# Edge scores of a graph kernel leave the gather ring by DMA beside the row store, where ScalarE copied them

## What is computed

```python
feat_all = einsum('ni,rhid->rnhd', inputs, conv_weights)
el = sum(feat_all[edge_type, edge_src] * attn_l[edge_type], -1)
er = sum(feat_all[edge_type, edge_dst] * attn_r[edge_type], -1)
e  = leaky_relu(el + er, 0.2)
alpha = softmax of e over the edges of one destination
h  = segment_sum(alpha[..., None] * feat_src_e, edge_dst) + h_bias
...
x = layernorm(x + L0(x)); x = layernorm(x + L1(x)); x = layernorm(x + L2(x)); x = layernorm(x + L3(x))
```

## Time and profile before

| | us |
|---|---|
| median of 3 runs | 2039.0 (2038.72 to 2039.45) |
| the profiled execution | 2046.73 |
| its span, first to last instruction | 2045.0 |
| first gather, last gather (start) | 157.4, 1001.2 |
| GpSimd busy | 523.6 |
| VectorE busy | 1154.6 |
| ScalarE busy | 779.0 |
| TensorE matmul busy | 1467.7 |

### The profile page before, as it was taken

The page is one execution under the profiler, slowest core; times in us unless marked ns, Lnnn a source line. Parts: engine busy times, 40 slices in busy tenths (PEclk is TensorE's granted clock), DMA queues, the critical chain, the costliest instruction groups (busy, mean ns, idle before and its releaser), DMA issues.

```text
span 2045.0 us, 22094 instructions
## 1 busy us (share of the span) xinstructions
PE 1467.7 (72%) x5398; PEld 742.5 (36%) x5398; DVE 1154.6 (56%) x2998; ACT 779.0 (38%) x1163; POOL 523.6 (26%) x517
## 2 busy tenths in 40 slices
PE   6895888755545555555239999798998789889640
PEld 3443544110001010010128777554444344544430
DVE  5404443777767677776599988752261350530636
ACT  1332433655545555555110000035773337156021
POOL 0005344556646656666400000000000000000022
PEclk9995555655555555555559999898999989999875
DMA  3534333445544444544509888200000100000022
GB/s 143 170 141 139 128 113 121 148 145 165 163 133 148 154 143 154 171 152 154 170 28 314 273 273 268 78 1 22 1 1 1 31 0 1 1 1 1 11 57 61
DMA packets 74860, 223.92 MB, mean 109 GB/s; under 512 B 17384, under 2 KB 26516, under 8 KB 74260
## 3 DMA queue, kind: packets, MB, share of 16 engines
q1 hardware_dynamic: 50804, 158.00, 21.7%
q0 software_dynamic: 23968, 64.77, 11.8%
HBM read 140.09 MB, written 82.63 MB: 109 GB/s over the span
## 4 chain that ended last, share of the span: by engine, by line
PE 39%; DVE 13%; issue 6%; DVEq 2%; ACT 1%; POOL 1%; DMA 0%; another core or an unknown queue 0%; SPq 0%; POOLq 0%
PE bank L1673 14%; PE bank L1612 11%; PE bank L1693 2%; PE bank L1745 2%; PE bank L1657 2%; DVE arena L1079 1%; DVE arena L1037 1%; PE bank L1742 1%; DVE adjacency L1044 1%; DVE arena L1038 1%; PE bank L1731 1%; PE bank L1641 1%; POOL arena L523 1%; PE bank L1756 1%; ACT arena L605 1%
## 5 line engine op out<-in xcount | busy, mean ns | idle before, releaser
L523 POOL DMA_INDIRECT arena<-feat_table,arena x469 | 486.8, 1038 | 456.7 <-issue 240.4
L1554 PE MATMUL bank<-arena 128*128 128x480 f16 x586 | 336.6, 575 | 270.8 <-DVE arena L1038 161.1
L605 ACT ACTIVATE arena<-bank 128x480 uint16<-128x480 f32 x586 | 332.6, 572 | 274.9 <-PE bank L1554 172.6
L1044 DVE TENSOR_TENSOR adjacency<-adjacency,arena 128x480 uint16 x586 | 235.7, 402 | 131.8 <-issue 90.8
L1673 PE MATMUL bank<-arena 128*128 128x472 f16 x1440 | 294.9, 369 | 12.0 <-DVE arena L1228 8.1
L531 POOL DMA_INDIRECT arena<-al_table,edge_ends x15 | 14.5, 965 | 977.9 <-DMA al_table<-arena 973.7
L1554 PEld LDWEIGHTS bank<-arena 128*128 128x128 f16 x586 | 60.8, 104 | 546.8 <-DVE arena L1038 283.7
L1612 PE MATMUL bank<-arena 128*128 x966 | 229.3, 393 | 0.8 <-issue 0.3
L1673 PEld LDWEIGHTS bank<-arena 128*128 128x128 bf16 x1440 | 142.7, 99 | 164.4 <-issue 18.4
L1038 DVE TENSOR_SCALAR arena<-iota,arena 128x480 f16<-128x480 f16 x586 | 201.4, 344 | 0.0
L1612 PEld LDWEIGHTS bank<-arena 128*128 128x128 f32 x966 | 175.3, 191 | 55.1 <-issue 33.2
(11 more groups left out here) (291 smaller groups left out, 1533.6 us busy)
## 6 DMA issues: line engine op xcount, KB each, us to landing
edge_rows<-arena SPq DMA_DIRECT2D x67, 910.0 KB
arena<-edge_rows SPq DMA_DIRECT2D x117, 520.0 KB, 4.6
feat_table<-arena SPq DMA_DIRECT2D x60, 260.0 KB, 2.1
arena<-feat_table,arena POOLq DMA_INDIRECT x469
arena<-in_w SPq DMA_DIRECT2D x1, 2048.0 KB, 9.7
arena<-in_xT SPq DMA_DIRECT2D x1, 1920.0 KB, 18.2
arena<-in_x SPq DMA_DIRECT2D x1, 1792.0 KB
xt_table<-arena SPq DMA_DIRECT2D x3, 528.0 KB, 3.2
```

The lines of the kernel that those rows point to most:

```text
L523: g.indirect_dma_start(out=SLOT[k][:, j, :], out_offset=None, in_=feat_t, in_offset=bass.IndirectOffsetOnAxis(ap=IE[:, GB * b + j:GB * b + ...
L605: a.activation(EV[st % AS].rearrange("p r k -> p (r k)"), PS[4 + st % 4][:, 0:R2 * KW], ACT.Copy)\
L1044: v.tensor_tensor(dst, dst, EV[st % AS], ALU.add).then_inc(s["a_add"], 1)
L1554: mm(PS[4 + st % 4][:, 0:R2 * KW], OHS[st % AS], OHK[st % AS], start=True, stop=True).then_inc(s["a_mm"], 1)
```

## The change

ScalarE's `collect` and all its calls are gone, with the numbers that spread them. For each batch SyncE issues, ahead of the row store and behind the same wait, a DMA that takes the 4 score columns of the slot (128 partitions x 7 pieces of 16 bytes) straight into `SUM`. Both DMAs count on one semaphore a slot, so each batch adds 32, and the helper `moved(k, batches)` tells what slot `k` has reached when so many batches have gone through. GpSimd waits for that alone, TensorE's two waits ahead of the lane groups and VectorE's ahead of the weighing become waits on the three slots' semaphores, and the first row load waits for the end of the step-score stage, `sc_mm`, where it waited for `collected`.

```diff
-GC_ER, GC_ET, GC_LOOP = 10, 2, 62
...
+        def moved(k, batches):
+
+            return 32 * ((batches + NSLOT - 1 - k) // NSLOT)
...
             for b in range(NGB):
                 k = b % NSLOT
                 sp.wait_ge(g_done[k], BATCH * (b // NSLOT + 1))
+                sp.dma_start(SUM[:, GB * b:GB * (b + 1), :], SLOT[k][:, :, D:FW]).then_inc(r_st[k], 16)
                 sp.dma_start(rows_b[:, GB * b:GB * (b + 1), :], SLOT[k]).then_inc(r_st[k], 16)
 
             for k in range(NSLOT):
-                sp.wait_ge(r_st[k], 16 * ((NGB + NSLOT - 1 - k) // NSLOT))
+                sp.wait_ge(r_st[k], moved(k, NGB))
...
                 if b == 0:
-                    sp.wait_ge(s["collected"], NGB)
+                    sp.wait_ge(s["sc_mm"], SC)
...
                 if b >= NSLOT:
-                    pool.wait_ge(r_st[k], 16 * (b // NSLOT))
-                    pool.wait_ge(s["collected"], b - NSLOT + 1)
+                    pool.wait_ge(r_st[k], 32 * (b // NSLOT))
...
-            def collect(b):
-
-                act.wait_ge(g_done[b % NSLOT], BATCH * (b // NSLOT + 1))
-                a.activation(SUM[:, GB * b:GB * (b + 1), :], SLOT[b % NSLOT][:, :, D:FW], ACT.Copy).then_inc(s["collected"], 1)
...
-                if g % 3 == 0 and g:
-                    collect(g // 3 - 1)
...
-                if c % 2:
-                    collect(GC_ER + c // 2)
...
-                    due = GC_ER + GC_ET + (GC_LOOP - GC_ER - GC_ET) * (AU * n + u + 1) // (A_N * AU)
-                    while got < due:
-                        collect(got)
-                        got += 1
...
-            pe.wait_ge(s["collected"], B_EARLY)
+            for k in range(NSLOT):
+                pe.wait_ge(r_st[k], moved(k, B_EARLY))
             pe.wait_ge(s["pool_link"], 3)
             for g in range(GR):
                 if g == G_EARLY:
-                    pe.wait_ge(s["collected"], NGB)
+                    for k in range(NSLOT):
+                        pe.wait_ge(r_st[k], moved(k, NGB))
```

More of the change, by code:

```diff
@@ L324, in build @@
         names = """bias_ready turn_cols kb_mm ld_rec ld_w0 ld_xt ld_at ld_e3 consts fields idx_mm idx_ev vl_done tab_mm tab_ev tab_st feat_mm
-            feat_ev diag_done bc_mm sel_free collected cmp_done ws_mm selr_ready djr_mm sel_ready fld_mm fld_ev steps_done a_oh a_mm a_ev a_add
+            feat_ev diag_done bc_mm sel_free cmp_done ws_mm selr_ready djr_mm sel_ready fld_mm fld_ev steps_done a_oh a_mm a_ev a_add
             pool_link lane_mm lane_ev flags_in flags_mm tail_ready tail_mm cin_ready cin_mm exp_ready exp_done
@@ L338, in build @@
         g3 = [sem(f"rows_gathered{i}") for i in range(len(GROUPS))]
-        r_st = [sem(f"rows_stored{i}") for i in range(NSLOT)]
+        r_st = [sem(f"rows_and_scores_moved{i}") for i in range(NSLOT)]
         REL = S3.rearrange("p a b -> p (a b)")[0:1, 0:RBLK - NRB].bitcast(I32)
@@ L609, in _ @@
                 a_evac(0, st)
-            got = GC_ER + GC_ET
             for n in range(A_N):
@@ L613, in _ @@
                     a_evac(n, AS + u)
-                    due = GC_ER + GC_ET + (GC_LOOP - GC_ER - GC_ET) * (AU * n + u + 1) // (A_N * AU)
-                    while got < due:
-                        collect(got)
-                        got += 1
             for st in range(AS + A_N * AU, STEPS):
                 a_evac(0, st)
-            for b in range(got, B_EARLY):
-                collect(b)
             for g in range(GR):
-                if g == G_EARLY:
-                    for b in range(max(got, B_EARLY), NGB):
-                        collect(b)
                 act.wait_ge(s["lane_mm"], g + 1)
@@ L1148, in _ @@
             for k in range(NSLOT):
-                dve.wait_ge(r_st[k], 16 * ((NGB + NSLOT - 1 - k) // NSLOT))
+                dve.wait_ge(r_st[k], moved(k, NGB))
             for i in range(RGRP):
```

## The result

| | before | after |
|---|---|---|
| median | 2039.2 us (2038.7 to 2048.1) | **2446.0 us** (2443.3 to 2448.2, 4 runs) |
| span of the profiled execution | 2045.0 | 2445.0 |
| last gather (start) | 1001.2 | 787.8 |
| first and last product of the key stage | 167.5, 344.3 | 165.9, 903.9 |
| first and last add of the count loop | 369.0, 979.2 | 928.2, 1390.5 |

The ratio is 1.198, with an interval of 1.195 to 1.202. The sign and the mechanism were as forecast (rival A), but the time is 176 us above the 2270 forecast and outside the range of 2020 to 2320. The key stage did 0.37 matmuls per us beside the train, where the sum took 1.35.

What follows compares the result with a forecast made beforehand. Gathers ended last, 17 us over the count loop; unbroken, they would slow the key stage to 723 and start the loop at 759: +237, rounded to +231, on the 2039.0 median gives 2270 us, range 2020 to 2320.

Steps and rivals of the forecast that it cites:

- rival A: The forecast itself: any unbroken gather train slows key stage and count loop until it ends; 2225 to 2320 us, chance 0.58.
- the sum: Second L1106 moves from 1007.3 to 1244: +237 us, rounded to +231 and added to the median of 2039.0.
- The bound and the mechanism: Gathers end last, 17 us over the count loop; waits for ScalarE break the trains and let other engines' sequencers recover.
- ScalarE's copies at nothing: Removing 67 copies on ScalarE, 14.6 us in all, was counted as no gain because ScalarE doesn't pace the loop.
- score transfers under cover: 67 added transfers on SyncE's queue: 10.2 us per slot against 17.5 available, so GpSimd shouldn't wait.
- The train's end, 743.7: 469 gathers at 1.25 us each from 157.4, landed at 747; at 1.33 us each, 784.
- The key stage's pace, 1.35 per us between 1.2 and 1.56: TensorE beside the train: 743 products left at 173 take 550 us, to 723.
- The loop's 2.3 us a step: Count loop's pace in slow stretches beside gathers: 19 steps in 44 us.
- Within about 2 us of the end of the run they are on time again: Count loop: VectorE's late steps recover about 2 us after a run of three gather batches, about 28 us, ends.
- my own last sentence: The forecast is wrong above all if a long train lets TensorE's sequencer recover.
- The loop and the rest: Count loop after the train: 440 us of steps plus 35 of turns, 759 to 1234, then 10.4 us to the second L1106.
- Rival C: Slow stretches don't grow with the train and come as often as now until gathers end at 747; 1970 us, chance 0.20.

Runs made afterwards that it cites:

- paced_2: Changed kernel, GpSimd also waiting ahead of a batch until ScalarE's ordinary work reached where `collect` stood; 2044.2 us against 2042.0 before on chip 6.
- train_beside_loop: Changed kernel with the first gather held until the key stage is done, so the train lies beside the count loop; 2377.6 us against 2047.0 before on chip 10.

## Why the prediction was wrong in size, point by point

- **The bound and the mechanism: right.** GpSimd gathers in one train without waiting for anyone, TensorE's key stage takes 738 us with idle time called "issue", and the loop has no slow stretch. paced_2 shows that nothing else in the change counts. That the sign came out right was also luck: on chips 5 and 14 kernels with this train were faster than before (1849 and 1842 us against 1892), and no row of one trace could tell on which sort of chip the result would be taken.
- **ScalarE's copies at nothing, score transfers under cover: right.** GpSimd never waited for a slot by the profile, and without the transfers the time is 4 us less.
- **The train's end, 743.7: 44 us early.** 1.25 us per gather was the cadence in short windows; over the train it is (787.8 - 155.8) / 468 = 1.35, just past my upper end of 1.33.
- **The key stage's pace, 1.35 per us between 1.2 and 1.56: the step that failed.** It was 0.37. With 229 of 743 matmuls done by 788, 514 were left. The nine microseconds that priced it were the first of a slow stretch, before the pace had settled; both bounds came from the same nine, so the range was no bound at all. The loop's 2.3 us a step has the same fault (5.0 measured in train_beside_loop), but didn't enter the sum of the forecast, in which no step of the loop lies beside the train.
- **"Within about 2 us of the end of the run they are on time again": wrong for a long train.** After the last gather at 787.8 TensorE goes on as before until 808; its next rows (and behind the x20 it is at pace):

```profile
808.11 0.17 PE L1501 MATMUL bank<-arena 128*128 x1 [2.62 <-issue]
815.95 0.61 PE L1487 MATMUL bank<-adjacency,ident 128*128 128x512 f16 x1 [7.67 <-DVE arena L978]
...
818.27 2.61 PE L1501 MATMUL bank<-arena 128*128 x20
```

  It is on time again at 816, 28 us after the gathers. In train_beside_loop VectorE's steps stay 4 to 6 us apart from 931.0 until 956.9, 26 us. Part of this time no DMA runs at all (796 to 807 in the changed kernel: four products in 11 us at 0 GB/s):

```profile
796.00:807.00 11.00, 0.68 (x4) 0.52 (x5) 0.00 (x0) 0.00 (x0) 0.00 (x0) 0.50 0.00 0
```

  So the state outlasts the traffic. This is also the answer to my own last sentence, on whether a long train lets a sequencer recover: it does not, and recovery is slower after it.
- **The loop and the rest: right.** 475 us forecast, 462 measured (928.2 to 1390.5). VectorE, beside the earlier trace rows:

```profile
1390.50 0.41 DVE L1028 TENSOR_TENSOR adjacency<-adjacency,arena 128x480 uint16 x1 [0.26 <-DVE adjacency L1028]
...
1401.26 0.67 DVE L1090 SCALAR_TENSOR_TENSOR arena<-arena 128x512 f32<-128x512 f32 x1
```

  The second L1090 comes 10.8 us after the loop, forecast 10.4, and has no idle time of 17.20 us ahead of it any more.
- **The sum with the measured terms:** train to 788, recovery to 816, the rest of the key stage and the 25 us stage to 928, loop and scans to 1401, against 1007.3: +394 of the 400 us between the two spans. The loop started 169 us later than forecast (759) and was 13 us shorter, so the second L1090 came 157 us later than forecast (1244). The other 19 us of the miss of 176 are the 6 that I rounded off the sum, and 13 by which the medians lie further apart (407) than these 394.
- **Rival C** was held at 0.20. On chips 5 and 14 its premise is the case: neither the key stage nor the loop slows beside an unbroken train. The Trainium skill, SBUF — State Buffer, "Who interferes with whom", by which a DMA never contends with a compute engine, agrees with those two chips. On the four others the trace does not agree, as far as GpSimd's gathers go: 76 matmuls in 200 us beside gathers that move 3 MB in all.

## What to carry to other kernels

A wait that looks like lost time can be what keeps other engines alive, so before taking one out, look at what runs while it waits. A slow stretch that ends soon can give the price of entering a state and not of staying in it; it must not be extended to a stretch seventy times as long with bounds from the same few microseconds. Look at whether its last rows are slower than its first. If GpSimd issues many indirect gathers beside fine-grained work, try a wait for a landing every few gathers, and measure on more than one chip: here it gained 3.8% on one and lost 3.0% on another.

## What the runs showed of the hardware

- **Chips differ.** One program, its gathers unbroken, took 1842 us on chip 14 and 2441 on chip 15; before took 1892 on two chips and 2012 to 2047 on four. Each chip was used on one occasion, and what sets them apart no run here shows. The granted clock (0.50 and 0.51 in these stages) and the DMA rate (111 GB/s) are the same.
- **A train of indirect gathers from GpSimd starves the sequencers of other engines** on those four chips, down to about a thirteenth of TensorE's pace (0.37 against 5 matmuls per us). VectorE's register instructions take 703 ns in the median where they took 75, and the add beside them 408 where it took 401. GpSimd's own issue doesn't suffer: 0.95 us as a median and 0.30 between two. The gathers' bytes (65 or 3 MB) and the small pieces (4 of 404 us) don't matter, and row stores aren't needed (30 gathers at the end of each program). Which part of an issue does it wasn't separated.
- **The state has a memory.** It takes 12 us of train to begin in the loop of before, about 18 us in the key stage (155.8 to 174) and 25 to 28 us in the last layer. It builds up over trains that are broken too little, and ends 26 to 28 us after a train of 630 us, though within about 2 us after one of 28. A pause of 2.1 us after each 7 gathers prevents it, one of 0.8 us doesn't.
